# A graph-convolution, attention and expert kernel on one core: the key/value products move into the degree stage, and the tile builds of the first pass get deeper buffers

## What is computed

```python
xn = layernorm(x)                                    # N x 256
deg_out = segment_sum(edge_weight, src); deg_in = segment_sum(edge_weight, dst)
norm = edge_weight * rsqrt(deg_out[src] * deg_in[dst] + 1e-12)
h6 = relu(segment_sum((xn @ W6)[src] * norm[:, None], dst) + b6)
h7 = relu(segment_sum((h6 @ W7)[src] * norm[:, None], dst) + b7)
gnn = h7 @ Wp + bp
k, v = LN(xn @ wk.T), LN(xn @ wv.T)                  # per head of 64, with scale and bias
kv = einsum('bhsd,bhse->bhde', k, v) / N             # linear attention: one 64x64 block a head
mix = einsum('bhsd,bhde->bhse', xn @ wq.T, kv) @ wo.T + bo
x = x + gnn + mix
x = x + LN(expert_ffn(LN(x)) + LN(x)) * gamma + beta # 2 of 8 experts, chosen once for all tokens
```

## Time and profile before

| | us |
|---|---|
| three runs, median (lowest to highest) | 3768.78 (3760.32 to 3772.62) |
| the profiled execution, its own time | 3763.83 |
| its span, first to last instruction | 3762.0 |
| front, to its last matmul | about 429 |
| from there to the first gather | 19 |
| pass 0 | about 448 to 2030 |
| between the passes | about 2030 to 2100 |
| pass 1 | about 2100 to 3333 |
| expert stage | about 3333 to 3762 |

### The profile page before, as it was taken

One profiled execution on the slowest core, in us unless ns is written; L12 is line 12 of the kernel. 1 busy time (PEld: TensorE's weight loads), 2 busy tenths in 40 slices (PEclk: granted clock), 3 DMA queues, 4 the chain that ended last, 5 costly groups with the idle time before them and its releaser, 6 DMA issues.

```text
span 3762.0 us, 52448 instructions
## 1 busy us (share of the span) xinstructions
PE 2974.0 (79%) x16152; PEld 2012.6 (53%) x16152; DVE 1794.8 (48%) x4526; ACT 1136.8 (30%) x4013; POOL 2162.5 (57%) x2090
## 2 busy tenths in 40 slices
PE   4565468878888888888885488788897887878998
PEld 4454335555555556555553256466565554655666
DVE  9999745556565555655542131322411244222334
ACT  6787453334443433433330010200100111002211
POOL 5776566666666666666664666566665666630000
PEclk8788869989999999999987689899898988998999
DMA  4210134445444444444445545455555554543221
GB/s 125 63 35 2 26 108 140 138 127 156 144 133 152 146 132 148 144 137 142 140 140 162 143 142 187 124 186 182 152 189 186 172 157 146 175 145 110 76 78 47
DMA packets 254147, 492.54 MB, mean 131 GB/s; under 512 B 61871, under 2 KB 135487, under 8 KB 253525
## 3 DMA queue, kind: packets, MB, share of 16 engines
q0 software_dynamic: 88704, 243.35, 22.8%
q1 hardware_dynamic: 158657, 239.29, 19.3%
q10 hardware_dynamic: 6500, 6.40, 0.5%
HBM read 376.56 MB, written 112.35 MB: 130 GB/s over the span
## 4 chain that ended last, share of the span: by engine, by line
PE 52%; DVE 17%; issue 10%; another core or an unknown queue 6%; ACT 4%; DMA 3%; POOL 3%; DVEq 2%; SPq 2%; ACTq 1%; POOLq 0%
PE ps L678 22%; PE ps L656 9%; DVE ab L1060 6%; PE ps L847 5%; PE ps L640 5%; PE ps L860 4%; DVE ab L1058 3%; POOL ringb L1908 2%; DMA ab<-in_x 2%; ACT ab L1683 1%; PE ps L603 1%; PE ps L619 1%; SPq L1969 1%; DVE mlb L1237 1%
## 5 line engine op out<-in xcount | busy, mean ns | idle before, releaser
L1908 POOL DMA_INDIRECT ringb<-t,src x1848 | 1852.5, 1002 | 1056.3 <-issue 487.8
L678 PE MATMUL ps<-xb,ab 125*128 125x256 f32 (+1 forms) x4700 | 1199.8, 399 | 85.8 <-issue 74.9
L678 PEld LDWEIGHTS ps<-xb,ab 125*128 125x128 f32 x4700 | 918.0, 199 | 336.9 <-issue 178.1
L656 PE MATMUL ps<-mlb 128*125 128x300 f32 x1260 | 482.5, 472 | 190.9 <-ACT side L1687 99.3
L1683 ACT ACTIVATE ab<-ps 125x250 f32 x724 | 293.6, 405 | 633.0 <-PE ps L656 366.0
L640 PE MATMUL ps<-ringb,Sb 128*32 128x257 f32 (+1 forms) x3696 | 334.4, 421 | 119.7 <-DVE Sb L1201 47.9
L656 PEld LDWEIGHTS ps<-mlb 128*125 128x125 f32 x1260 | 225.2, 203 | 351.2 <-issue 303.2
L562 PE MATMUL ps<-ab 128*50 128x125 f32 x3228 | 243.8, 304 | 184.9 <-ACT ab L1610 126.1
L1270 DVE TENSOR_TENSOR ab<-ab,side 125x50 f32 x724 | 177.8, 246 | 400.7 <-ACT side L1687 197.2
L1881 POOL TENSOR_TENSOR ab<-ab,wn 128x100 f32<-128x100 f32 x201 | 274.1, 1368 | 128.1 <-DVE ab L1058 128.1
L562 PEld LDWEIGHTS ps<-ab 128*50 128x50 f32 x3228 | 204.0, 142 | 224.5 <-DVE ab L1060 192.9
(11 more groups left out here) (227 smaller groups left out, 2681.2 us busy)
## 6 DMA issues: line engine op xcount, KB each, us to landing
ad<-ab SPq DMA_DIRECT2D x210, 312.5 KB
ab<-ad SPq DMA_DIRECT2D x210, 312.5 KB
ringb<-t,src POOLq DMA_INDIRECT x1848
x2t<-mlb SPq DMA_DIRECT2D x13, 500.0 KB
xb<-x2t SPq DMA_DIRECT2D x13, 500.0 KB, 8.3
xb<-in_x SPq DMA_DIRECT2D x10, 625.0 KB
t<-xb SPq DMA_DIRECT2D x10, 625.0 KB
kvb<-t SPq DMA_DIRECT2D x50, 125.0 KB
```

What stands on the lines that cost most here:

```text
L656: e.matmul(PS[(2, 7, 4, 5)[bank_of(t)]][0:R, 0:HR], low[:, slot_of(t), :], high[:, slot_of(t), :], start=True, stop=True).then_inc(s_bld, 1)
L678: ins = e.matmul(PS[3][:, 0:wd], lhs, X[0:R, k, 0:wd], start=k == 0, stop=k == NT - 1)
L1908: e.indirect_dma_start(msg[:, slot * QT + k, 0:width], None, table, bass.IndirectOffsetOnAxis(src[:, t:t + 1], 0)).then_inc(s_g[slot], 16)
```

## The change

- **Front.** After the matmuls of batch `KV_AT[i]` (20, 23, 27, 30, ... 196, on average 3.6 batches apart) PE transposes node tile i straight from the normalised rows in `xb`. ACT copies it behind its weights of the next batch (`kv_rows`), PE multiplies by the key/value weights behind its batch two later (`kv_product`), and ACT copies the raw product out behind its weights of the batch three later (`kv_raw`). SP stores both, the raw product in a new DRAM array `kvd`. The centring of the weights (three DVE instructions, L1098 to L1102, that stood behind the front) comes at batch 17.
- **Pass 0, keys and values.** SP loads the raw product (250 KB a tile, before 125 KB of rows), ACT squares it from SBUF, and the rest is as before, a step earlier for the sum. Transposes, products and ACT's copy are gone.
- **Pass 0, builds.** Three sets of one-hot slots in place of two (HG = 3), `hots(s + 2)` in place of `hots(s + 1)`, three banks in place of two, nine `side` slots in place of six; `first_column` is added two steps after the build; `weigh_lo` stands ahead of all evictions; `clear` moves three steps back, into the chunk's own step 2, and only tile 15 of a chunk waits for it; the dense products start one step later; the stores of A are issued two a step in steps 1 to 5 of a chunk in place of one a step in 0 to 9.
- `mlb` grows, and the scratch for GpSimd's transfer descriptors is set to 8192 bytes, half of the default 16384.

```diff
--- before.py
+++ after.py
 RF = 3
 FIRST = 6
 KV = 4
+HG = 3
+MLW = 3940
+FRONT_EX = 2400
+LATE_CLEAR = 15
 MLS = 3
 NS = 4
 TURN = 3
-SD = 6
+SD = 9
...
+KV_AT = [20 + i * 18 // 5 for i in range(NT)]
...
-        MULT_AT[0].setdefault((_d + 1) * PD + 1 + _k * (PD - 2) // NT, []).append((_d, _k))
+        MULT_AT[0].setdefault((_d + 1) * PD + 2 + _k * (PD - 2) // NT, []).append((_d, _k))
...
+        mlb = sb("mlb", [P, MLW])
+        Mb = mlb[:, 0:HG * MLS * HR].rearrange("p (s c) -> p s c", c=HR)
+        Lb = mlb[:, HG * MLS * HR:HG * MLS * (HR + R)].rearrange("p (s c) -> p s c", c=R)
...
-            return s % 2 * MLS + BUILD_AT[0][s].index(t)
+            return s % HG * MLS + BUILD_AT[0][s].index(t)
...
-            return t % 2 + 2 * (t >= tile_of(DY))
+            return (4, 5)[t % 2] if t >= tile_of(DY) else (2, 7, 5)[t % 3]
+
+        def banks(t):
+            return 2 if t >= tile_of(DY) else 3
...
+            def kv_transposed(i):
+                e.wait_ge(s_nx, i + 1)
+                if i >= 1:
+                    e.wait_ge(s_kxc, i)
+                for h in range(2):
+                    ins = e.transpose(PS[4][:, h * P:h * P + R], X[0:R, i, h * P:(h + 1) * P], ident[0:R, 0:R])
+                ins.then_inc(s_ktr, 1)
+
+            def kv_product(i):
+                e.wait_ge(s_kxc, i + 1)
+                if i == 0:
+                    e.wait_ge(l_wts, 16 * N_WTS)
+                    e.wait_ge(s_cen, 3)
+                if i >= 1:
+                    e.wait_ge(s_krc, i)
+                for h in range(2):
+                    ins = e.matmul(PS[5][0:R, :], xT[:, i % 2, h, :], wkv[:, h, :], start=h == 0, stop=h == 1)
+                ins.then_inc(s_kmm, 1)
...
+                if c in KV_AT:
+                    kv_transposed(KV_AT.index(c))
+                if c - 2 in KV_AT:
+                    kv_product(KV_AT.index(c - 2))
...
-                if ph == 0:
-                    e.wait_ge(l_kx[k], 16 * loads_of(i + 1, k))
-                    if i >= 1:
-                        e.wait_ge(s_kxc, i)
-                    if hidden_issued(s) >= 1:
-                        e.wait_ge(s_hadd, hidden_issued(s))
-                    for h in range(2):
-                        ins = e.transpose(PS[4][:, h * P:h * P + R], xt[0:R, k, h * P:(h + 1) * P], ident[0:R, 0:R])
-                    ins.then_inc(s_ktr, 1)
-                if ph == 1:
-                    e.wait_ge(s_kxc, i + 1)
-                    if i == 0:
-                        e.wait_ge(s_cen, 3)
-                    if i >= 1:
-                        e.wait_ge(s_kv, 5 * i - 2)
-                    for h in range(2):
-                        ins = e.matmul(PS[5][0:R, :], xT[:, k, h, :], wkv[:, h, :], start=h == 0, stop=h == 1)
-                    ins.then_inc(s_kmm, 1)
...
-                if kv_copied(s) >= 1:
-                    e.wait_ge(s_kxc, kv_copied(s))
...
-                if t >= 2:
-                    e.wait_ge(s_ev, t - 1)
-                    if r0_before(t - 1):
-                        e.wait_ge(s_c0, r0_before(t - 1))
+                n = banks(t)
+                if t >= n:
+                    e.wait_ge(s_ev, t - n + 1)
+                    if r0_before(t - n + 1):
+                        e.wait_ge(s_c0, r0_before(t - n + 1))
...
                     return
-                ps3 = PS[5][0:R, :].rearrange("p (a d) -> p a d", d=64)
-                kk = kvs[0:R, :].rearrange("p (a d) -> p a d", d=64)
-                if ph == 2:
...
-                    e.tensor_tensor(kk, ps3, h8[0:R, 3, :].unsqueeze(2).to_broadcast([R, 8, 64]),
-                                    ALU.mult).then_inc(s_kv, 1)
+                    e.tensor_tensor(kvs[0:R, :].rearrange("p (a d) -> p a d", d=64),
+                                    kin[0:R, k, :].rearrange("p (a d) -> p a d", d=64),
+                                    h8[0:R, 3, :].unsqueeze(2).to_broadcast([R, 8, 64]), ALU.mult).then_inc(s_kv, 1)
...
-                if builds_before(s - 1):
-                    e.wait_ge(s_bld, builds_before(s - 1))
-                n, o, c0 = len(b), s % 2 * MLS, TS + b[0]
+                if builds_before(s - HG + 1):
+                    e.wait_ge(s_bld, builds_before(s - HG + 1))
...
-                    if (s + 1) % PD == 0 and 1 <= (s + 1) // PD < DY:
-                        clear((s + 1) // PD)
-                    for t in BUILD_AT[0].get(s - 1, ()):
+                    if s % PD == 2 and 1 <= s // PD < DY:
+                        clear(s // PD)
+                    for t in BUILD_AT[0].get(s - 2, ()):
                         first_column(t)
-                    hots(s + 1)
+                    hots(s + 2)
...
+            def kv_rows(i):
+                k = i % 2
+                e.wait_ge(s_ktr, i + 1)
+                if i >= 2:
+                    e.wait_ge(s_kmm, i - 1)
+                    e.wait_ge(l_xs[k], 16 * loads_of(i - 1, k))
+                e.activation(xT[:, k, :, :], PS[4][:, 0:2 * P].rearrange("p (h c) -> p h c", h=2)[:, :, 0:R],
+                             ACT.Copy).then_inc(s_kxc, 1)
+
+            def kv_raw(i):
+                k = i % 2
+                e.wait_ge(s_kmm, i + 1)
+                if i >= 2:
+                    e.wait_ge(l_kr[k], 16 * loads_of(i - 1, k))
+                e.activation(raw[0:R, k, :], PS[5][0:R, :], ACT.Copy).then_inc(s_krc, 1)
...
+                if c - 1 in KV_AT:
+                    kv_rows(KV_AT.index(c - 1))
+                if c - 3 in KV_AT:
+                    kv_raw(KV_AT.index(c - 3))
...
-                    e.wait_ge(s_ktr, i + 1)
-                    if i >= 2:
-                        e.wait_ge(s_kmm, i - 1)
-                        e.wait_ge(l_xs[k], 16 * loads_of(i - 1, k))
-                    e.activation(xT[:, k, :, :], PS[4][:, 0:2 * P].rearrange("p (h c) -> p h c", h=2)[:, :, 0:R],
-                                 ACT.Copy).then_inc(s_kxc, 1)
-                if ph == 1:
-                    e.wait_ge(s_kmm, i + 1)
-                    e.activation(sq[0:R, :], PS[5][0:R, :], ACT.Square).then_inc(s_ksq, 1)
+                    e.wait_ge(l_kx[k], 16 * loads_of(i + 1, k))
+                    if i >= 1:
+                        e.wait_ge(s_kv, 5 * i - 4)
...
+                if k == 0 and d >= DY:
+                    e.wait_ge(s_az, d + 1)
+                if k == 0 and 2 <= d < DY:
+                    e.wait_ge(s_mul, 5 * (d - 1))
+                    e.wait_ge(l_as[place], 16 * PA * loads_of(d - 1, place))
+                if k == LATE_CLEAR and d < DY:
+                    e.wait_ge(s_az, d + 1)
                 if k == 0:
-                    e.wait_ge(s_az, d + 1)
...
-                    for t in BUILD_AT[0].get(s, ())[:1]:
-                        evict(t)
                     weigh_lo(s + 1)
-                    for t in BUILD_AT[0].get(s, ())[1:]:
+                    for t in BUILD_AT[0].get(s, ()):
...
+
+            def kv_stored(i):
+                k = i % 2
+                e.wait_ge(s_kxc, i + 1)
+                e.dma_start(xtd[i // 4].rearrange("p (h n) -> p h n", h=2)[:, :, i % 4 * R:(i % 4 + 1) * R],
+                            xT[:, k, :, :]).then_inc(l_xs[k], 16)
+                e.wait_ge(s_krc, i + 1)
+                e.dma_start(kvd[i * R:(i + 1) * R, :], raw[0:R, k, :]).then_inc(l_kr[k], 16)
+
+            for c in range(len(BATCHES)):
+                if c in T1_AT:
+                    rows_stored(T1_AT.index(c))
+                if c - 4 in KV_AT:
+                    kv_stored(KV_AT.index(c - 4))
...
-                    e.wait_ge(s_ktr, i - 1)
-                e.dma_start(xt[0:R, k, :], tile_rows(t1, i)).then_inc(l_kx[k], 16)
+                    e.wait_ge(s_kv, 5 * (i - 2) + 3)
+                e.dma_start(kin[0:R, k, :], kvd[i * R:(i + 1) * R, :]).then_inc(l_kx[k], 16)
...
-                if s % PD < PA and 1 <= s // PD <= DY:
-                    store_A(s // PD - 1, s % PD)
+                if 1 <= s % PD <= PA // 2 and 1 <= s // PD <= DY:
+                    for p in range(2 * (s % PD) - 2, 2 * (s % PD)):
+                        store_A(s // PD - 1, p)
                 i, ph = divmod(s - FIRST, KV)
-                if ph == 1 and 0 <= i < NT - 2:
-                    kv_load(i + 2)
-                if ph == 1 and 0 <= i < NT:
-                    e.wait_ge(s_kxc, i + 1)
-                    e.dma_start(xtd[i // 4].rearrange("p (h n) -> p h n", h=2)[:, :, i % 4 * R:(i % 4 + 1) * R],
-                                xT[:, i % 2, :, :]).then_inc(l_xs[i % 2], 16)
+                if ph == 0 and 1 <= i < NT - 1:
+                    kv_load(i + 1)
...
-    nc = bacc.Bacc("TRN2", target_bir_lowering=False, num_devices=1)
+    nc = bacc.Bacc("TRN2", target_bir_lowering=False, num_devices=1, dynamic_dma_scratch_size=8192)
```

More of the change, by code:

```diff
@@ L80 @@
 BATCHES = [(t, min(DB, T - t)) for t in range(0, T, DB)]
+KV_AT = [20 + i * 18 // 5 for i in range(NT)]
+assert KV_AT[-1] + 4 < len(BATCHES)
+T1_AT = [19 + 9 * b for b in range(NB)]
 def size_of(d):
```

(8 more changed lines are left out.)

78 lines of the change are left out of this document (42 added, 36 removed).

## The result

The changed kernel took 3739.48 us in the median of 8 runs (3732.03 to 3745.69), the kernel before 3770.7 us (8 runs): a ratio of 0.992, 95% interval 0.9895 to 0.9945. The forecast was 3630 us. The profiled execution has a span of 3737.6 us against 3762.0.

The account below looks back on a forecast made before the run. VectorE bounds the front, with ACT nearly as full; in pass 0 no engine is full, a ring of waits delays PE. 3763.8 + 55 (front) - 192 (pass 0) = 3627, about 3630 us; range 3550 to 3725.

Parts of the forecast that it names:

- Front, +55: Front: PE's added transposes and products and ACT's copies lengthen it by 55 us, between +36 and +200.
- rival C: Front: becomes PE's at the low clock, costing up to 200 us; total 3777 us, slower than before; chance 0.08.
- the rule (36): Front: activity lifts PE's slow clock state, so the cost would be nearer the full-clock +36 us.
- Between and scratch, 0: Between front and pass 0, moving the centring saves nothing; halving the descriptor scratch costs nothing.
- Pass 0, work, -122.5: Pass 0: PE loses 122.5 us of transposes and products, its busy time going from 1305 to 1183 us.
- Pass 0, waits: Pass 0: loosened waits cut PE's idle time from 277 to 190 us, giving 1373; 1390 taken, 192 less than now.
- a ring that the change takes apart: Pass 0: build, eviction, first column, one-hots, weights, next build wait on each other; the ring spans four steps instead of two.
- Pass 0, the other bound, 1312: Pass 0: POOL's 984 gathers with their issue time need 1312 us even if POOL never waits.
- B: Pass 0: only the work goes, waits stay or are replaced; pass 0 1460 us, total 3700 us; chance 0.20.
- D: Both passes: smaller scratch makes gathers dearer, 1.4 us each instead of 1.03; total 4085 us; chance 0.04.
- E: Better than forecast: pass 0 at POOL's 1312 us and the front at +36; total 3535 us; chance 0.08.
- Pass 1, 0: Pass 1: keeps its instructions, so nothing changes, staying at about 1230 us.

Follow-up runs that it names:

- both_later: Changed kernel with both PSUM copies of the front a batch later, on a long chip: 3749.37 us, 0.9908 of before.
- short chip: Name for groups of runs in which the kernel before took about 3555 us; a name of groups and not more.
- long chips: Name for groups of runs in which the kernel before took 3770 to 3790 us, the first comparison among them; a name of groups and not more.
- the first comparison: The changed kernel against the kernel before, 8 runs each, on the long chips: 3739.48 against 3770.7 us, 0.992.
- the first group: First follow-up runs, on a short chip; among them the changed kernel with the builds' part taken back, only the moved products left: 3517.47 us, 0.9896 of before.
- builds_alone: Kernel before with only the builds' part, without the third bank: 3492.14 us, 0.9826 of before on a short chip; 3790.59 us, 1.0007 on a long one.
- the halved gathers: Two of four gathers left out per group of pass 0, short chip: changed kernel 3422.32 us (0.961), moved products only 3474.78 us (0.9769).
- after_again: The changed kernel itself, run again beside the kernel before on a short chip: 0.9889 of before.
- slots_order: Kernel before with third slot set, one-hots two steps ahead, small scratch, and ACT's next weights ahead of all evictions, long chip: 3746.96 us, 0.9934 of before.
- after_2: The changed kernel itself, run once more on a long chip: 3780.45 us, 0.9963 of before.
- narrow_gathers: Changed kernel with pass 0's gathers from the seventh group on cut to 130 of 258 columns, long chip: 3771.33 us, 0.9952 of before.

## Why the prediction was wrong

*Front, +55.* Right in size: +57, with the wait of 1.77 us before the raw copy measured at 1.75, and the clock up to 0.93, so that the low-clock price (rival C) did not come. Its parts were not right, and here there was some luck. The forecast at full clock had 33 us for the batches behind `norm_x` and 3 for those beside it, and 19 more as a mix. Measured by the starts of L1058 and its successor L1066, the last 100 batches cost 27 us (2.152 us each against 1.882; from 260.8 to 476.0, at a clock of 0.99) and those up to batch 91 cost 20 (236.5 against 216.5, at a clock of 0.86), where the raw copies waited 41.2 us for PE, up to 9.2 at a time. In both_later the late batches are nearly back at the old pace (1.910), and what is left of the cost stands in the early ones.

By the Trainium skill (TensorE: Matmul & The Clock Gate, Part 1) activity lifts the throttled state, and the trace agrees: 0.84 with PE busy 233 of 401 us, 0.93 with 333 of 458. The cost that the prediction drew from the rule (36) did not come out: 57.

*Between and scratch, 0.* Right: from the start of the front's last batch on PE to the first gather 20.4 us (505.15 - 484.71) against 20.2; scratch 1.0012, on a short chip.

*Pass 0, work, -122.5.* Too large. PE's busy time from first to last gather fell from 1297.0 to 1214.5, by 82 us; on short chips from 1243 to 1150, by 93. The removed groups measured 122 us, but the groups' products rose from 167 to 184 us and the hidden ones from 61 to 67 in the traces of the long chips. Why they rise was not tested.

*Pass 0, waits: "PE's idle time is 1582 - 1305 = 277; less about 95, plus 10, is 190".* This is the step that failed. From gather to gather it was 1564 - 1297 = 267 and became 262. I had read two rows, 99.3 us for ACT's `side` and 43.8 of "issue", as places in a ring that the change takes apart. On the long chips much of it is PE's own signals coming late, as the bunch at 550 us shows, and whoever is next in order is named: before builds PE stood 190.9 us there and 99.9 on a short chip, with the same instructions. Taking slots and banks apart does not shorten that part (190.9 to 183.2). Where the bunches don't occur the waits do shorten: on short chips PE's wait before builds fell from 99.9 to 34.1 us and VectorE's for evictions from 200 to 26. But PE's idle time as a whole stayed there too, 171 and 172 us, since the gathers then hold the pass.

*Pass 0, the other bound, 1312.* Right in kind, and it decides on the short chips: 1321 to 1330 measured. A gather costs 1.04 to 1.05 us in the mean of these passes (1021.8 and 1030.1 / 984) instead of 1.031. But I took 1390 between the two bounds from a start of 1582. On short chips the start is 1414, only 90 above the floor, so the two parts can't add: 84 and 51 alone, 93 together, against a front of 57. On long chips the pass stays 150 to 180 above the floor, and the late signals are what the traces show in between.

*The rivals.* B, only the work goes and the waits stay or are replaced, is what happened in the first comparison: -122 forecast, -88 measured, since the work fell by 82. It had 0.20. The argument written under it, that `hots(s + 2)` still waits for the builds of step s - 1, shows in the trace (VectorE's one-hots wait 146 us for PE, 100.3 + 46.2). C, D and E did not come. The expectation in the first group that named loosened waits as worthless fell with builds_alone and the halved gathers.

*Pass 1, 0.* Right: +3.

**Left open.** Why PE's signals come late in some groups of runs with many gathers issued, and not in others, and whether that is a property of a chip at all. Both kinds move the same packets. The recording is one candidate: every execution here was recorded, and in pass 0 of the changed kernel the long trace holds 8710 records of semaphore updates, the short one (after_again) 23240, with 4013 and 4010 in the front. Records are lost where the gathers run, and a lost record is one way in which a releaser comes to have no name; whether the recording also holds PE's signals up, no run without it can tell. Instruction fetch is another, since its queues stand among those of the DMA engines that carry the gathers; the Trainium skill (Runtime: NRT & Kernel Launch) says that sequential prefetch hides it, and no run here was made on it; the instruction queues moved the same packets on both kinds (141, and 147 or 148). Against it: PE's build at 532.64 starts 0.17 us after the end of ACT's eviction, so PE had this instruction at hand. The Trainium skill (SBUF — State Buffer, Who interferes with whom) says that DMA never contends with a compute engine; the runs here show PE, ACT and VectorE held up by something that goes away with half the gathers and not with half their bytes, but not by what path. Nor is it settled why builds_alone gives nothing on a long chip (1.0007) where slots_order gives 0.66% in another group.

## What to carry to other kernels

Before adding the gains of two edits to one stage, work out the floor of the engine that neither touches, with all it pays between two instructions (here 984 x 1.35 us): a stage 90 us above it can give 90 once, and whoever of the two costs something elsewhere is the one to leave out. A wait whose named releaser itself stood idle just before is not a wait for that engine: look in the timeline at what all the others were waiting for. And leaving out half of a suspected stream is a far quicker test than taking a schedule apart: it separated floor, ring and disturbance in one run of each kind.

## What the runs showed of the hardware

One and the same program takes 3555 us in some groups of runs and 3770 to 3790 in others; the front is the same in both (its last batch starts on PE at 427.89), and the difference lies in the passes with gathers (1414.0 and 1226.7 us against 1564.2 and 1290.8). Signals of PE can come 8 to 27 us after the modelled end of its work, in a bunch, and the traces in which they do hold under half as many records of semaphore updates as the others in the passes with gathers, where all gathers run. A gather of 258 columns cost POOL 1.035 us in the mean (after_2, 1016.89 / 983), one of 130 columns 1.031 (narrow_gathers, 1014.73 / 984): its price on POOL is that of the instruction, not of the bytes. Cutting the gathers' descriptor scratch to 8192 bytes changed nothing on a short chip (1.0012).
